# A convolution tap as a TensorE product with a diagonal matrix, and a new order of steps

## The reference

```python
g = einsum('th,ehi->tei', x, Wg); u = einsum('th,ehi->tei', x, Wu)
mlp_out = einsum('tei,eih->teh', silu(g) * u, Wd)
routed = einsum('te,teh->th', cw[:, :4], mlp_out) + (cw[:, 4:5] + cw[:, 6:7]) * x + cw[:, 7:8] * relu(x)
shared = causal depthwise convolution of x over 4 rows of time, weights conv_w (4 x 128), plus conv_b
return routed + shared
```

## Time and profile before

| | us |
|---|---|
| median of three runs | 186.35 |
| lowest, highest | 185.25, 188.18 |
| the profiled run | 186.44 |
| span of the profiled run, first to last instruction | 184.2 |
| mean granted clock of TensorE | 0.991 of full |

### The profile page before, as it was taken

One profiled execution on the slowest core, in us unless ns is written; L12 is line 12 of the kernel. 1 busy time (PEld: TensorE's weight loads), 2 busy tenths in 40 slices (PEclk: granted clock), 3 DMA queues, 4 the chain that ended last, 5 costly groups with the idle time before them and its releaser, 6 DMA issues.

```text
span 184.2 us, 5548 instructions
## 1 busy us (share of the span) xinstructions
PE 165.1 (90%) x1802; PEld 113.8 (62%) x1802; DVE 160.8 (87%) x448; ACT 135.2 (73%) x309; POOL 110.8 (60%) x200
## 2 busy tenths in 40 slices
PE   6868996896889999999999999999999989999693
PEld 6856773555555657757875677567457546755472
DVE  6848698988889999999999998998999998588891
ACT  2159744687568978999887997989777779875661
POOL 7894954416562774959019885575676178844562
PEclk9999999999999999999999999999999999999969
DMA  5941123222220320122213003212320000000001
GB/s 159 325 188 45 48 71 83 62 72 62 62 71 7 80 80 23 43 63 68 59 30 86 4 18 93 76 33 62 89 59 5 28 4 5 30 4 0 30 2 57
DMA packets 17796, 11.00 MB, mean 60 GB/s; under 512 B 2388, under 2 KB 17108, under 8 KB 17768
## 3 DMA queue, kind: packets, MB, share of 16 engines
q1 hardware_dynamic: 17768, 10.66, 19.8%
HBM read 3.10 MB, written 1.05 MB: 22 GB/s over the span
## 4 chain that ended last, share of the span: by engine, by line
PE 61%; DVE 15%; issue 13%; ACT 7%; POOL 1%; DVEq 0%; ACTq 0%; POOLq 0%
PE max_pair L975 11%; PE pv_bank L975 10%; PE ffn_bank L975 10%; PE self_bank L975 9%; PE soft_pair L975 8%; DVE negmax L857 5%; PE cross_bank L975 5%; PE pv_bank L1139 2%; PE self_bank L979 2%; ACT xn L613 1%; ACT probs L648 1%; DVE stats L751 1%; PE ffn_bank L1188 1%; PE ffn_bank L979 1%; DVE shift L777 1%
## 5 line engine op out<-in xcount | busy, mean ns | idle before, releaser
L857 DVE TENSOR_REDUCE negmax<-max_pair 128x4 f32<-128x1024 f32 (+1 forms) x48 | 58.3, 1215 | 3.6 <-PE max_pair L975 3.2
L648 ACT ACTIVATE probs<-soft_pair 128x1024 f32<-128x1024 f32 x46 | 47.1, 1024 | 9.3 <-PE soft_pair L975 9.1
L520 POOL TENSOR_SCALAR_AFFINE_SELECT probs<-probs 128x512 f32<-128x512 f32 (+1 forms) x48 | 38.1, 808 | 12.1 <-ACT probs L648 11.9
L975 PE MATMUL pv_bank<-probs,vs 128*32 128x128 f32 (+1 forms) x512 | 23.9, 329 | 0.2 <-POOL probs L520 0.2
L975 PE MATMUL max_pair<-causal,picks 64*128 64x128 bf16 (+1 forms) x192 | 15.3, 238 | 5.2 <-DVE negmax L857 3.7
L975 PEld LDWEIGHTS pv_bank<-probs,vs 128*32 128x32 f32 x512 | 14.4, 109 | 8.8 <-issue 1.7
L975 PE MATMUL soft_pair<-qs,ks 64*128 64x256 bf16 (+1 forms) x244 | 17.9, 245 | 1.4 <-DVE maxparts L864 0.8
L975 PE MATMUL max_pair<-ks,qs 64*128 64x128 bf16 (+1 forms) x256 | 18.4, 242 | 0.0
L494 POOL TENSOR_TENSOR rstd<-vareps,exponent 128x2 f32<-128x2 f32 x24 | 16.9, 706 | 2.0
L486 POOL TENSOR_SCALAR vareps<-mv 128x2 f32<-128x2 f32 x24 | 5.2, 219 | 21.2 <-DVE mv L765 20.4
L975 PE MATMUL ffn_bank<-loaded,x3T 128*128 128x8 f32 (+1 forms) x52 | 17.1, 424 | 0.6 <-ACT x3T L674 0.5
(11 more groups left out here) (199 smaller groups left out, 398.0 us busy)
## 6 DMA issues: line engine op xcount, KB each, us to landing
ks<-kparts SPq DMA_DIRECT2D x48, 64.0 KB, 2.0
qs<-qparts SPq DMA_DIRECT2D x48, 64.0 KB, 2.0
out_dram<-result SPq DMA_DIRECT2D x8, 128.0 KB, 1.8
loaded<-packed_dram SPq DMA_DIRECT2D x1, 768.0 KB, 7.2
loaded<-packed_dram SPq DMA_DIRECT2D x1, 640.0 KB, 8.3
qs<-maxparts SPq DMA_DIRECT2D x32, 4.0 KB
loaded<-packed_dram SPq DMA_DIRECT2D x1, 462.5 KB, 5.7
loaded<-packed_dram SPq DMA_DIRECT2D x2, 192.0 KB, 3.4
```

The lines of the kernel that those rows point to most:

```text
L520: nc.gpsimd.affine_select(out=v, in_=v, compare_op=ALU.is_ge, fill=0.0, base=0, pattern=[[0, n], [1, P]], channel_multiplier=-1).then_inc( ...
L648: nc.scalar.activation(probs[b.par][g][:, k, :], pair_of_soft(b, u)[:, :], ACT.Exp).then_inc(exp_done, 1)
L857: nc.vector.tensor_reduce(maxima, max_pair[:, :].rearrange("p (u h k) -> p u h k", u=2, h=n), AX.X, ALU.max, negate=True).then_inc(max_rea ...
L975: return nc.tensor.matmul(out, lhsT, rhs, start=start, stop=stop, skip_group_check=True)
```

## The change

Tap 3 leaves VectorE. A 128 x 128 matrix `last_tap` with the weights of tap 3 on its diagonal is made once by a ScalarE instruction (`diagonal`), and `ffn_conv` multiplies `x3T` by it into the same down bank, two products per batch beside the two with the identity. `conv_done` now counts two taps per batch. The lists of steps of all five engines are written anew; most steps keep their neighbourhood and many change places by a few. The lines of the lists that follow are those that the text below speaks of; the rest of the lists is left out.

```diff
 "sp"
-        hi_q.4.0 send_max.3.0 lo_q.4.0 mid_k.4.0 mid_q.4.0 zero_max.4.0 mid_k.5.0 lo_k.5.0 zero_max.5.0 hi_k.5.0
+        send_max.1.1 mid_k.3.0 hi_q.3.0 lo_k.3.0 lo_q.3.0 mid_q.3.0 send_max.2.0 send_max.2.1 zero_max.4.0
+        mid_k.4.0 hi_q.4.0 send_max.3.0 mid_q.4.0 lo_k.4.0 lo_q.4.0 hi_k.4.0 hi_k.5.0 zero_max.5.0 send_max.3.1
+        mid_k.5.0 store_out.0.0 hi_q.5.0 mid_q.5.0 lo_k.5.0 lo_q.5.0 zero_max.6.0 send_max.4.0 send_max.4.1
...
 "pool"
-        bias.0.0 rbias.0.0 bias.1.0 rstd1.3.0 lo_k.0.0 rstd2.0.0 clear_v.0.2 bias.2.0 clear_v.0.3 lo_q.0.0
+        lo_k.1.0 rstd2.2.0 lo_q.1.0 clear_v.0.2 clear_v.0.3 mask.0.0 routes.0.0 rstd2.3.0 lo_k.2.0 mask.0.1
...
 "act"
+        norm1.5.0 mid_q.1.0 max_hi.0.0 norm2.2.0 xnT.4.0 hi_k.2.0 vs.2.0 diagonal.0.0 x2nT.2.0 act_q.4.0 exp.0.0
...
 "dve"
-        clear.0.0 clear.0.3 stats1.0.0 var1.0.0 clear.0.1 norm1.0.0 clear.0.4 clear.0.2 stats1.1.0 var1.1.0
+        clear.0.0 clear.0.3 stats1.0.0 var1.0.0 clear.0.1 norm1.0.0 clear.0.4 clear.0.2 clear.0.5 phi_q.0.0
+        stats1.5.0 phi_k.1.0 shift2.0.0 phi_k.2.0 phi_q.1.0 phi_q.2.0 kvsum.1.0 kvsum.2.0 var1.5.0 div1.1.0
...
-        gate.5.1 times_up.5.1 route.6.4 x2.7.0 route.6.5 stats3.7.0 route.6.6 var3.7.0 gate.6.0 skip.6.0
+        tap.6.1 gate.5.1 times_up.5.1 route.6.0 route.6.1 route.6.2 x2.7.0 stats3.7.0 var3.7.0 route.6.3
...
-        tap.7.1 tap.7.2 tap.7.3 finish.6.0 finish.7.0
+        route.7.6 times_up.7.1 tap.7.1 skip.7.0 tap.7.2 finish.6.0 finish.7.0
...
 "pe"
-        self_q1.1.0 self_q1.2.0 self_o_t.0.0 self_kv.1.0 self_proj.0.0 self_kv.2.0 self_x_t.3.0 self_sum.1.0
+        self_q1.1.0 self_o_t.0.0 self_q1.2.0 self_proj.0.0 self_kv.1.0 self_kv.2.0 self_x_t.3.0 self_sum.1.0
...
+        last_tap = sb("last_tap", [P, P])
...
+            def diagonal(_, __):
+
+                act.wait_ge(consts, 3)
+                wait_for(act, "conv")
+                nc.scalar.activation(last_tap[:, :], ident[:, :], ACT.Identity, scale=w["conv"][:, KC - 1:KC]).then_inc(last_tap_ready, 1)
...
                 else:
-                    dve.wait_ge(conv_done, b.count(KC - 1, j - 1))
+                    dve.wait_ge(conv_done, b.count(KC - 2, j - 1))
...
             def ffn_conv(b, _):
 
-                pe.wait_ge(conv_done, b.count(KC - 1, KC - 1))
+                pe.wait_ge(conv_done, b.count(KC - 2, KC - 2))
+                pe.wait_ge(last_tap_ready, 1)
                 pe.wait_ge(hidT_done if b.c < B - 2 else hid0_done, b.count(1, 1) if b.c < B - 2 else b.count(2, 2))
                 for t in range(T):
                     mm(bank_of_ffn(b, "down")[:, t * C:(t + 1) * C], convT[b.par][:, t * P:(t + 1) * P], ident[:, :], start=t == 0, stop=False)
+                    mm(bank_of_ffn(b, "down")[:, t * C:(t + 1) * C], x3T[b.par][:, KC - 1 + t * P:KC - 1 + (t + 1) * P], last_tap[:, :],
+                       start=False, stop=False)
```

More of the change, by code:

```diff
@@ L46 @@
[L46 to L50, removed]
@@ L75 @@
[L75 to L79 removed]
+        xnT.0.0 act_q.0.0 act_kv.0.0 hi_k.0.0 norm1.2.0 xnT.1.0 xnT.2.0 mid_k.0.0 vs.0.0 o1T.0.0 act_q.1.0
@@ new lines @@
+        rest_k.2.0 reduce.0.4 stats2.3.0 reduce.0.5 var2.3.0 max_mid.0.1 reduce.1.0 phi_k.4.0 reduce.1.1
+        rest_q.2.0 shift2.3.0 kvsum.4.0 reduce.1.2 phi_q.4.0 max_mid.1.0 reduce.1.3 reduce.1.4 div1.4.0
+        rest_k.3.0 reduce.1.5 var1.6.0 div1.4.1 div1.4.2 reduce.2.0 div2.0.0 div2.0.1 max_mid.1.1 reduce.2.1
+        rest_q.3.0 x2.0.0 stats3.0.0 x1.4.0 var3.0.0 reduce.2.2 shift3.0.0 reduce.2.3 max_mid.2.0 stats2.4.0
+        var2.4.0 rest_k.4.0 reduce.2.4 shift2.4.0 stats1.7.0 reduce.2.5 route.0.0 route.0.1 route.0.2 reduce.3.0
@@ new lines @@
+        phi_k.5.0 shift1.6.0 var1.7.0 max_mid.2.1 gate.0.0 phi_q.5.0 times_up.0.0 reduce.3.1 kvsum.5.0 div2.1.0
+        div2.1.1 reduce.3.2 div1.5.0 div1.5.1 div1.5.2 rest_q.4.0 x2.1.0 route.0.3 max_mid.3.0 shift1.7.0
+        reduce.3.3 x1.5.0 route.0.4 stats2.5.0 tap.0.1 reduce.3.4 stats3.1.0 gate.0.1 var2.5.0 var3.1.0
+        rest_k.5.0 times_up.0.1 route.0.5 tap.0.2 route.0.6 reduce.3.5 phi_k.6.0 shift2.5.0 phi_q.6.0 skip.0.0
+        reduce.4.0 max_mid.3.1 shift3.1.0 div2.2.0 kvsum.6.0 reduce.4.1 div2.2.1 finish.0.0 div1.6.0 div1.6.1
@@ new lines @@
+        div1.6.2 reduce.4.2 rest_q.5.0 x2.2.0 x1.6.0 reduce.4.3 stats2.6.0 max_mid.4.0 var2.6.0 rest_k.6.0
+        gate.1.0 times_up.1.0 reduce.4.4 route.1.0 stats3.2.0 shift2.6.0 route.1.1 route.1.2 gate.1.1 route.1.3
+        var3.2.0 route.1.4 tap.1.1 route.1.5 route.1.6 times_up.1.1 reduce.4.5 skip.1.0 tap.1.2 phi_k.7.0
+        reduce.5.0 max_mid.4.1 div2.3.0 kvsum.7.0 shift3.2.0 reduce.5.1 div2.3.1 finish.1.0 phi_q.7.0 reduce.5.2
+        div1.7.0 rest_q.6.0 div1.7.1 x2.3.0 div1.7.2 stats3.3.0 reduce.5.3 max_mid.5.0 gate.2.0 var3.3.0
@@ new lines @@
+        pv.2.1 max.4.0 maxrow.3.1 ffn_hid_t.0.0 self_sum.6.0 out_t.2.0 max.4.1 soft.3.1 cross_norm_t.5.0
+        ffn_conv.0.0 ffn_down.0.0 self_out.6.0 o2_t.2.0 max.4.2 soft.3.2 ffn_x_t.1.0 cross_q2.5.0 self_o_t.6.0
+        o_proj.2.0 soft.3.3 max.4.3 self_proj.6.0 ffn_router.1.0 cross_k_v.6.0 maxrow.4.0 ffn_gate_up.1.0
+        self_x_t.7.0 soft.3.4 max.4.4 self_q1.7.0 ffn_gate_up.1.1 soft.3.5 max.4.5 pv.3.0 self_kv.7.0
+        cross_norm_t.6.0 pv.3.1 soft.4.0 max.5.0 ffn_hid_t.1.0 out_t.3.0 cross_q2.6.0 maxrow.4.1 self_sum.7.0
@@ L154 @@
+        ffn_gate_up.5.0 ffn_x_t.6.0 pv.7.1 ffn_router.6.0 out_t.7.0 ffn_gate_up.5.1 o2_t.7.0 ffn_gate_up.6.0
+        o_proj.7.0 ffn_hid_t.5.0 ffn_gate_up.6.1 ffn_conv.5.0 ffn_down.5.0 ffn_x_t.7.0 ffn_router.7.0
+        ffn_gate_up.7.0 ffn_gate_up.7.1 ffn_hid_t.6.0 ffn_conv.6.0 ffn_down.6.0 ffn_hid_t.7.0 ffn_conv.7.0
+        ffn_down.7.0
     """,
```

189 lines of the change are left out of this document (82 added, 107 removed).

## The result

| | before | after |
|---|---|---|
| median, us | 186.28 (4 runs) | 190.91 (4 runs) |
| lowest, highest | 185.25, 188.18 | 190.76, 191.61 |
| span of the profiled run | 184.2 | 189.0 |
| mean granted clock of TensorE | 0.991 | 0.982 |

The ratio is 1.0255, 95% interval 1.0212 to 1.0298. Medians are over all runs, while ratios and intervals leave out executions more than 1.5% above the fastest of their kernel. The forecast was 185.6 us, with a range of 182.3 to 188.8 us; the measured time lies above it.

A forecast was written before the change was run, and what follows sets the result against it. TensorE was taken to be on the path in the full stretch from 60 to 111 us, with VectorE full too. The terms +1.0 - 0.9 + 0.6 - 1.5 = -0.8 us gave 185.6 us, range 182.3 to 188.8 us.

The forecast's parts named there:

- New order elsewhere: Whole order, mainly TensorE's 10.7 us idle before 60 us: a seventh of it gained, -1.5 us, bounds -3 and +1.
- three moves towards the first scores and one against: self_proj.0 before self_kv.1, two vs clears after lo_q.1, shift2.0 before phi_k.2; against: clear.0.5 ahead of stats1.1.
- The text's own sign of failure: If the first score comes later, the -1.5 us for the order, called the softest term, fails.
- 60 to 111 us: Full middle stretch, TensorE on the path: products of ffn_conv.0 and .1 add 2 x 0.49 = +1.0 us, bounds -1.8 to +1.0.
- 111 to 160 us: Three pairs of products (+1.5) against three taps (-1.9), gaps on TensorE: -0.9 us, bounds -1.9 and +1.5.
- The two waits for convT: TensorE's loads waited twice for convT between 111 and 160 us, 0.9 us in total; that wait should go.
- Tail: Last batches: added products at the lower clock delay the drain, VectorE's var3.7 comes earlier: +0.6 us, bounds 0 and +1.2.
- Products on the path everywhere: Rival: products cost time at every ffn_conv, +4.3 us, and the order gains nothing: 190.7 us, chance 0.1.
- VectorE sets the pace: Rival: VectorE, not TensorE, limits the middle, so removed taps pay: -4.1 us, 182.3 us, chance 0.2.
- The low clock moves: Rival: the tail's lowered clock misses it (-1.7 us, 183.9 us) or covers conv.7 too (near 187 us), chance 0.15.
- the waiting would pass to the next one: VectorE's long taps: time above 0.46 us is waiting on GpSimd, inherited by the next instruction, so each frees only 0.4 us.
- the signs it named: convT lines on VectorE fall about 5 us, ffn_conv shows eight records in some 1.0 us, no TensorE wait for convT.

The follow-up runs named there:

- e1: Kernel after with the old lists of steps, only tap.b.3 taken out and the diagonal put before x2nT.2: 186.81 us, ratio 1.0026.
- e2: Kernel before (old computation, three taps on VectorE, no added products) with the new lists of steps: 191.11 us, ratio 1.0263.
- e9: New computation, old order until batch 3's first scores, then new with gate.0.0, times_up.0.0 behind reduce.3.1 and x1.5.0 before reduce.3.3: 188.24 us.
- e13: Kernel after with lo_k.0 before rstd2.0, picks.0 behind lo_q.0, and clear.0.5 back behind var1.3: 190.72 us, ratio 1.0149.
- e16: Kernel after with picks.0 before rstd1.3, lo_k.0 behind rstd1.3, and clear.0.5 behind var1.3: 190.96 us, ratio 1.0209.
- e14: e13 with TensorE's self_out.3 also moved behind max.0.0, as in the old order: 191.75 us, ratio 1.0287.
- e17: e16 with TensorE's self_out.3 also moved behind max.0.0, as in the old order: 193.33 us, ratio 1.0266.
- e6: New computation with all lists in the new order up to the first scores of batch 3 and the old order after: 197.18 us.
- e7: Kernel after with SyncE's list of transfers alone in the old order: 206.50 us, ratio 1.1123.
- e11: e1 with the last tap left out altogether, neither on VectorE nor as products: 185.82 us, ratio 0.9990.
- e12: e1 with VectorE's third tap kept beside the products, so the last tap counts twice: 188.52 us, ratio 1.0159.
- e10: New computation, old order up to the first scores of batch 5 and new order for the rest: 188.38 us, ratio 1.0066.

## Why the prediction was wrong, step by step

**New order elsewhere, -1.5 us, bounds -3 and +1: this step failed,** by its sign and by its bounds. It is +4.1 us (190.91 against e1's 186.81), or +4.6 us with the old computation (e2): some 2 us between the first scores of batches 3 and 5, of which moving three steps gives 1.0 to 1.4 back (e9), and some 2.2 us before batch 3, where a stop of 2.25 us is followed by 6 us or more at the lower clock. I took the 10.7 us of idle time of TensorE before 60 us as room that a better order could use, and named three moves towards the first scores and one against. What I didn't do is follow TensorE's own list and the transfers to `max.0.0`. No run tests those four moves one by one. The moves that the runs and rows led to are others, which I had not listed: `gate.0.0` ahead of `reduce.3.1` is shown to cost (e9); `picks.0` ahead of `lo_k.0` is worth little (e13, e16), and `self_out.3` ahead of `max.0.0` nothing that was gained by undoing it (e14, e17). Which moves make the longer stop stays open. In an order this tight (e6, e7 and e13 to e17 all missed a gain) the bounds should have reached further on the slow side than on the fast one. The text's own sign of failure, a later first score, came: 30.35 against 29.43 us, one execution of each.

**60 to 111 us, +1.0.** By e1 it is about +0.5 (from 1.0 us ahead at reduce.3.0 to 0.55 us ahead at reduce.5.0). The price of four records, 0.49 us, was right within 0.14 us.

**111 to 160 us, -0.9.** Mis-sized with the wrong sign: e1 goes from 0.55 us ahead of before at reduce.5.0 to 0.8 us behind it at result.4 (158.54 against 157.73), +1.4 us for the products of three batches. The two waits for convT did vanish, but the relief of VectorE was worth 0.2 us there (52.52 us in e11, 52.76 before). TensorE's gaps of 3.1 us took the products in the new order (52.92 us in the kernel after, 52.66 in e2) and not in the old (54.12 in e1, 52.52 in e11).

**Tail, +0.6.** From result.4 to the last result e1 is 0.4 us shorter (23.34 against 23.73). It lacked a term: the tap removed ahead of `ffn_conv.7` is worth some 0.7 us (e12), which I had counted at nothing. Also the halved clock of the earlier trace rows is gone in e1 and after; `gate_up.7` takes 1.96 us in both, 2.60 us before.

**The change without the order,** 1.0 - 0.9 + 0.6 = +0.7 us, came out at +0.3% or 0.5 us (e1). That is luck: behind reduce.3.0 the three terms measure +0.5, +1.4 and -0.4, together +1.4 us, two of them with the wrong sign, and the rest is that e1's profiled run reached reduce.3.0 1.0 us earlier under the same lists, and the clock that e1 had whole more often.

**The rivals.** "Products on the path everywhere" gave 190.7 us, almost the measured time, and its mechanism is refuted for this kernel: products for taps change nothing in the new order (e2 against after), and 4.0 us were lost before the first of them ran. The right number of a wrong reason. In the old order it has something: 0.7 to 2.0 us for the products, on the path from 111 to 160 us. "VectorE sets the pace" is out by e11. "The low clock moves" is the one that came true in part: it left the tail, which I had priced at -1.7 us, and appeared at 30 to 37 us for 1.5 to 3 us. It is not the new order's alone: e9, e10 and e11 each have one halved stretch while they follow the old one, at 14 to 17, 44 to 47 and 29 to 32 us. I had it move only inside the tail.

**The taps.** The group on convT fell from 24 instructions and 15.5 us to 16 and 9.3 us, more than the 5 us that the prediction gave as a sign. All of VectorE's instructions, added up line by line, fell by as much, from 180.3 to 174.2 us (174.3 in e1); only its busy time fell less, by 3.8 us (4.9 us in e1), since records overlap. No group of two-input instructions grew by more than 0.7 us, and `phi_q`, `phi_k` and `shift` fell. The prediction cited the Trainium skill (GPSIMD Engine Reference, Specifications) for the contention of GpSimd with such VectorE instructions, and added itself that the waiting would pass to the next one; the sums show nothing of that. Its other citation (Perfetto Trace Analysis, Identifying the Most-Contended Engine), by which loads busy 69% left TensorE room, held for the products in the new order, which took 3 us of idle time, and not in the old one, where they cost 0.7 to 2.0 us. Of the signs it named, `ffn_conv` has its eight records in 0.90 us; one wait for convT is left, of 0.6 us, in the last batch.

## What to carry to other kernels

- Where a change edits an instruction and the order of everything, run each alone first: two runs split this one, and the number of a rival that fits is no proof of its reason.
- Judge a new order by following the list of the engine on the path to its first milestone, with the transfers it waits for. Work done earlier than the transfer lands leaves one long stop in place of several short ones, and a lowered clock can follow it, which cost 1 to 3 us in these runs.
- A removed instruction is worth its length only where the engine behind it waits, here almost only in the last batch.
